# First attention: idle products in front of TensorE's waits, clearings and a first gate moved

## The chip, the cores and the metric

The kernel runs on one core of a Trainium2 chip. A core has a matrix engine (TensorE, PE in the profile), a vector engine (VectorE, DVE), an activation engine (ScalarE, ACT), a general engine (GpSimd, POOL) and a queue that issues transfers (SyncE, SP). The engines run their own instruction streams and wait for each other through semaphores. The metric is the device time of one launch in microseconds (us), and less is better.

## The reference

Six sublayers are added one after another to x (32 sequences of 64 tokens, 512 wide, so 2048 tokens), each on the layer norm of x. The change touches the first three:

```python
# 1: latent attention, 32 heads, latent width 4
C_q, C_kv = xn @ Wq_d + bq_d, xn @ Wkv_d + bkv_d
q = (C_q @ W_qk + b_qk).reshape(b, s, 32, 4)
attn = softmax(einsum('bqhd,bkd->bhqk', q, C_kv) / 2)
x += einsum('bhqk,bkhd->bqhd', attn, C_kv @ Wv_u + bv_u) @ Wo + bo
# 2: cross attention to ctx, 32 heads of 16 over 8 groups, mask added
x += softmax(xn_g @ ctx_g^T / 4 + mask) @ ctx_g
# 3: linear layer with 4 rank-8 experts, the expert by argmax of the gate logits
x += xn @ W_up^T + one_hot(argmax(xn @ gate_w^T + bias)) * lora(xn)
```

Then come a polynomial gated layer with a feed-forward part (4), one more attention (5) and a feed-forward layer with a latent branch (6). None of their code is changed.

## The kernel before

x lies in SBUF as 16 tiles of 128 tokens (`NT` = 16), in chunks of four tiles (`NC` = 4, `TC` = 4). Weights and activations are split into a high and a low fp16 half, and `mm3` (L116 to L118) multiplies them with three products. The order of each engine's work is written out by hand.

**Stage A, the first attention** (`stage_a`, until about 202 us). A unit is 16 heads of one tile; there are N = 32 units, eight in a chunk, n = 8c + j. TensorE's loop runs over n and issues `scores(n+1)` (L1118), `attend(n-2)` (many products of 10 columns, L116 to L118 into `a_p_v`), `scores_t(n)` (L1153), then the "front" work of the next chunk and the output work of the last one by the table `ring` (T: turn a normed tile, L: latents, V: values, Q: queries, Z: turn the result, O or P: output product; Y stands for Z by tiles in the last chunk), and last `turn_top(n+1)` (L1130). The other engines follow in the same order: VectorE takes the row maximum (`peak`, L603) and norms the result (`norm_z`), ScalarE does `shift` (L908), the exponential and the high half, GpSimd the low half (`low_p`, L435). On VectorE `spread` (L573) writes the masked keys of the next chunk and `low_query` (L595) the low half of a query block, which a later Q on TensorE waits for.

`keep_warm(times)` (L1137) issues products of 128 x 96 by 512 bf16 columns of an identity into `p_m`, whose rows 0 to 95 nobody reads: idle products, whose result is thrown away. Before the change 14 stand at the start (`EARLY_WARM`) and `light(c, j)` products behind the front work of an iteration, 0, 2 or 4.

GpSimd's `next_step(m)` prepares the second attention between the units: m = 0 and 1 clear `vn[0]` and `vn[1]` (L477), m = 2 writes a column of constants (L482), and later steps split its first keys and values.

**Stage B, the second attention** (`part_b`, about 202 to 367 us). It has again 32 units with the same kind of loop from n = -2: `turn` (L110), `scores`, `peak` (L1355), `shift` (L1526), `turn_p` (L1538), `attend`. `p_v`, the fourth bank of `p_y`, takes the results of `attend`. Stages A and B are separate blocks, and all engines meet between them.

**Stage C, the linear layer** (`part_c`, about 361 to 440 us). For a tile t, TensorE turns it (`trans`), forms gate logits and expert columns (`aux`) and the base product (`main`, twelve products of 512 columns); VectorE's `gate(t)` (five small instructions, L1639 to L1649) picks the expert, ScalarE's `high_z` and VectorE's `low_z` (L1655) split the picked columns, TensorE turns them (`turn_z`, L1775) and adds them (`delta`, L1781). `trans`, `aux` and `main` of tile 0 are issued inside stage B. Their results lie in other banks than `p_v`, but `main(1)` writes the bank of `p_v`.

## Time and profile before

| | |
|---|---|
| median of 3 runs | 1196.1 us (1193.16 to 1198.43) |
| the profiled execution's own time | 1192.04 us |
| its span | 1190.3 us |
| mean granted TensorE clock | 0.956 |
| PE busy | 1110.0 us, 93% of the span |
| DVE busy | 689.0 us, 58% |
| ACT busy | 492.6 us, 41% |
| POOL busy | 375.8 us, 32% |
| chain that ended last, by engine | PE 70%, DVE 9%, issue 2%, ACT 1% |

### The profile page before, as it was taken

How to read it: one execution, taken by the hardware profiler on the slowest of the kernel's cores; microseconds unless marked ns; L12 is line 12 of the kernel's file. 1: busy time of each engine (PE TensorE's matmuls, PEld its weight loads, DVE VectorE, ACT ScalarE, POOL GpSimd, SP SyncE). 2: the span in 40 equal slices, each digit the busy share in tenths (PEclk: the TensorE clock that was granted, in tenths of full speed). 3: DMA queues.
4: the chain of work that ended last, by engine and by line, in shares of the span. 5: the costliest groups of instructions: out<-in, count | busy, mean ns of one | idle time of the engine just before them, and what ended most of it. 6: DMA issues, size and time to landing. Idle time of an engine off the chain costs nothing.

```text
span 1190.3 us, 23660 instructions
## 1 busy us (share of the span) xinstructions
PE 1110.0 (93%) x9380; PEld 594.2 (50%) x9380; DVE 689.0 (58%) x1221; ACT 492.6 (41%) x871; POOL 375.8 (32%) x339
## 2 busy tenths in 40 slices
PE   7778996999998989999999999999989899999996
PEld 3444553677775444444444444444555544444442
DVE  6787775588887775335314412531389923656565
ACT  4465673788864644222212211221266622223221
POOL 2255465566651320000460160000043400415063
PEclk8888886799998999999999999999999999999998
DMA  7000000111120211310020010000000000000001
GB/s 242 2 2 4 18 15 9 41 47 45 44 68 4 83 47 43 107 62 1 21 81 1 0 53 0 1 1 1 0 12 10 1 1 1 18 18 26 9 29 43
DMA packets 29011, 35.91 MB, mean 30 GB/s; under 512 B 5882, under 2 KB 20499, under 8 KB 28788
## 3 DMA queue, kind: packets, MB, share of 16 engines
q1 hardware_dynamic: 27506, 34.53, 9.2%
q8 instruction: 67, 1.10, 0.4%
q10 hardware_dynamic: 1410, 0.06, 0.1%
q14 instruction: 28, 0.23, 0.1%
HBM read 30.24 MB, written 4.19 MB: 29 GB/s over the span
## 4 chain that ended last, share of the span: by engine, by line
PE 70%; DVE 9%; issue 2%; ACT 1%; POOL 0%; DVEq 0%; POOLq 0%; ACTq 0%
PE p_up L116 11%; PE p_up L117 11%; PE p_up L118 11%; PE p_y L116 9%; PE p_y L118 9%; PE p_y L117 9%; PE p_y L1538 3%; PE p_up L110 2%; DVE e_den L2257 2%; PE p_up L1526 1%; PE p_up L1503 1%; DVE wd_lo L103 1%; DVE st L188 1%; PE p_up L1508 1%; PE p_y L110 1%
## 5 line engine op out<-in xcount | busy, mean ns | idle before, releaser
L1949 DVE TENSOR_TENSOR d_h_low<-d_hf,d_h_high 128x512 f16<-128x512 f32 (+1 forms) x40 | 27.9, 697 | 205.1 <-ACT d_h_high L2038 205.1
L116 PE MATMUL p_up<-d_xt_high,wd_hi 128*128 128x512 f16 (+1 forms) x352 | 133.4, 379 | 2.9 <-PE p_y L118 1.5
L117 PE MATMUL p_up<-d_xt_low,wd_hi 128*128 128x512 f16 (+1 forms) x352 | 133.4, 379 | 0.0
L118 PE MATMUL p_up<-d_xt_high,wd_lo 128*128 128x512 f16 (+1 forms) x352 | 133.4, 379 | 0.0
L170 ACT ACTIVATE d_sg<-p_up 128x512 f32<-128x512 f32 (+1 forms) x40 | 23.8, 594 | 212.8 <-PE p_up L118 212.7
L116 PE MATMUL p_y<-wd_hi,d_h_high 128*128 128x512 f16 (+1 forms) x272 | 103.1, 379 | 0.0
L117 PE MATMUL p_y<-wd_lo,d_h_high 128*128 128x512 f16 (+1 forms) x272 | 103.1, 379 | 0.0
L118 PE MATMUL p_y<-wd_hi,d_h_low 128*128 128x512 f16 (+1 forms) x272 | 103.1, 379 | 0.0
L435 POOL TENSOR_TENSOR a_pt_low<-a_ex,a_pt_high 128x1024 f16<-128x1024 f32 x32 | 68.1, 2127 | 80.3 <-ACT a_pt_high L924 80.2
L138 POOL TENSOR_SCALAR wd_raw<-wd_raw 128x1156 f32<-128x1156 f32 x8 | 25.1, 3140 | 207.1 <-DVE d_h_low L1949 207.1
L2219 POOL TENSOR_TENSOR wd_hi<-wd_hi,e_den 128x1024 f32<-128x1024 f32 x16 | 30.5, 1909 | 147.7 <-DVE e_den L2259 147.7
L2549 DVE TENSOR_TENSOR d_h_low<-d_hf,d_h_high 128x512 f16<-128x512 f32 x32 | 28.6, 893 | 66.1 <-ACT d_h_high L2647 66.1
L116 PE MATMUL p_up<-d_xt_high,wf_hi 128*128 128x512 f16 x160 | 61.2, 382 | 0.0
L117 PE MATMUL p_up<-d_xt_low,wf_hi 128*128 128x512 f16 x160 | 61.1, 382 | 0.0
L118 PE MATMUL p_up<-d_xt_high,wf_lo 128*128 128x512 f16 x160 | 61.0, 381 | 0.0
L116 PEld LDWEIGHTS p_up<-d_xt_high,wd_hi 128*128 128x128 f16 (+1 forms) x352 | 35.3, 100 | 44.7 <-issue 3.0
L2640 ACT ACTIVATE d_sg<-p_up 128x512 f32<-128x512 f32 x32 | 19.1, 596 | 88.9 <-PE p_up L118 88.9
L118 PEld LDWEIGHTS p_up<-d_xt_high,wd_lo 128*128 128x128 f16 (+1 forms) x352 | 35.3, 100 | 40.7
L117 PEld LDWEIGHTS p_up<-d_xt_low,wd_hi 128*128 128x128 f16 (+1 forms) x352 | 35.3, 100 | 40.1
L1294 POOL TENSOR_TENSOR wd_lo<-wd_lo 128x512 f16<-128x512 f32 x30 | 34.7, 1157 | 45.7 <-ACT wd_lo L1437 41.1
L116 PE MATMUL p_y<-wf_hi,d_h_high 128*128 128x512 f16 x128 | 48.5, 379 | 0.1
L117 PE MATMUL p_y<-wf_lo,d_h_high 128*128 128x512 f16 x128 | 48.5, 379 | 0.0
(340 smaller groups left out, 2890.6 us busy)
## 6 DMA issues: line engine op xcount, KB each, us to landing
wd_raw<-in_w_d SPq DMA_DIRECT2D x16, 616.0 KB, 3.7
wd_raw<-in_w_f SPq DMA_DIRECT2D x8, 578.0 KB, 3.8
X<-in_x SPq DMA_DIRECT2D x4, 1024.0 KB, 12.3
wd_lo<-in_ctx_t SPq DMA_DIRECT2D x128, 32.0 KB
out_x<-wd_raw SPq DMA_DIRECT2D x16, 256.0 KB, 2.0
wd_lo<-in_ctx SPq DMA_DIRECT2D x32, 64.0 KB, 2.4
wd_raw<-in_w_c SPq DMA_DIRECT2D x1, 1096.0 KB, 12.5
wd_hi<-in_Wo SPq DMA_DIRECT2D x1, 1024.0 KB
```

The lines of the kernel that those rows point to most:

```text
L110: last = nc.tensor.transpose(ps[:, 128 * k:128 * k + 128], xn[:, 128 * k:128 * k + 128], held.ident[:])
L116: nc.tensor.matmul(ps, st[0], mv[0], start=start, stop=False)
L117: nc.tensor.matmul(ps, st[0], mv[1], start=False, stop=False)
L118: return nc.tensor.matmul(ps, st[1], mv[0], start=False, stop=stop)
L138: nc.gpsimd.tensor_scalar(raw, raw, WS, None, ALU.mult).then_inc(done, 1)
L435: nc.gpsimd.tensor_tensor(pt[1][:, n % 3, :, :], ex[:, n % 2, :, :], pt[0][:, n % 3, :, :], ALU.subtract).then_inc(pt_ready, 1)
L1294: nc.gpsimd.tensor_tensor(bd[1][:, h, :, 128 * i:128 * i + 128], ks.rearrange("p (k n) -> p k n", k=KB), bd[0][:, h, :, 128 * i:128 * i + ...
L1538: last = nc.tensor.transpose(p_t[:, q, 128 * k:128 * k + 128], prob[:, n % 2, 8 * q + 2 * k:8 * q + 2 * k + 2, :] .rearrange("p h k -> p ( ...
L1949: nc.vector.tensor_tensor(hid[1][0:n, d % NH, :], value, hid[0][0:n, d % NH, :], ALU.subtract).then_inc(h_ready, 1)
L2219: nc.gpsimd.tensor_tensor(prob[:, t % 3, :, :], prob[:, t % 3, :, :], den[:, t % 2, :].rearrange("p (j a) -> p j a", a=1).broadcast_to([12 ...
L2257: nc.vector.tensor_reduce(den[:, b, :], prob[:, t % 3, :, :], AX.X, ALU.add).then_inc(sum_ready, 1)
L2549: nc.vector.tensor_tensor(hid[1][:, f % NH, :], sq[:, f % 2, :], hid[0][:, f % NH, :], ALU.subtract).then_inc(h_ready, 1)
```

## The change

Idle products are added in stage A: 30 in place of 14 at the start; 7 behind `scores(0)` and 6 behind `turn_top(0)`; 7 in place of 2 at the end of iterations 4 and 6; 6 at the head of iteration 7; 2 ahead of the front work of iterations 12, 13, 20 and 21; 5 and 4 ahead of `attend` in the two iterations after the last unit; 5 ahead of the third output block of the last chunk and 2 ahead of its fourth. In stage B a `keep_warm` of its own (128 x 128 by 512 columns, into `p_v`) is added: 8 ahead of `turn(0)`, 5 ahead of `turn(1)`, 5 ahead of `shift(0)`. GpSimd's clearings move from behind `low_p` of units 12, 14 and 16 to those of units 10, 18 and 19. Stage C's `gate(0)` moves from the head of stage C on VectorE into stage B's iteration 31, `high_z(0)` on ScalarE ahead of `norm(2)`, and on TensorE `trans(2)`, `aux(1)` and `main(1)` go ahead of `turn_z(0)`, with a wait for stage B's last result (`held.b_outputs`) ahead of `main(1)`.

```diff
@@ -343,7 +343,9 @@
         def bank(use):
             return p_f[:, bank_of[use], :]
 
-        EARLY_WARM = 14
+        EARLY_WARM = 30
+        WAITS = {4: 7, 6: 7}
+        TAIL = {N: 5, N + 1: 4}
         held.rs_steps = 4 * NC - 2
 
         def light(c, j):
@@ -477,7 +479,7 @@
                         nc.gpsimd.memset(vn[m], 0.0).then_inc(next_clear, 1)
                     elif m == 2:
                         pool.wait_ge(next_clear, 2)
-                        pool.wait_ge(pt_ready, N - 15)
+                        pool.wait_ge(pt_ready, N - 12)
                         for r, h in halves:
                             nc.gpsimd.memset(vn[0][r, :, :, h, DH:DH + 1], AS).then_inc(next_clear, 1)
                         pool.wait_ge(next_clear, 4)
@@ -515,8 +517,8 @@
                         pool.wait_ge(next_low, 2)
                 for n in range(N):
                     low_p(n)
-                    if n in (12, 14, 16):
-                        next_step((n - 12) // 2)
+                    if n in (10, 18, 19):
+                        next_step({10: 0, 18: 1, 19: 2}[n])
                     if 24 <= n < 31:
                         next_step(n - 21)
                     if n in (2, 5):
@@ -1186,27 +1188,39 @@
                     if use[0] == "Q" and use[2] == 1:
                         fold_bvo(range(2, 4))
                 scores(0)
+                keep_warm(7)
                 turn_top(0)
+                keep_warm(6)
                 for use in second:
                     front(use)
                 for n in range(N + 2):
+                    if n == 7:
+                        keep_warm(6)
                     if n + 1 < N:
                         scores(n + 1)
+                    if n in TAIL:
+                        keep_warm(TAIL[n])
                     if n >= 2:
                         attend(n - 2)
                     if n < N:
                         scores_t(n)
+                        if n // 8 in (1, 2) and n % 8 in (4, 5):
+                            keep_warm(2)
                         for use in chunk_uses(n // 8, n % 8):
                             front(use)
-                        keep_warm(light(n // 8, n % 8))
+                        keep_warm(WAITS.get(n, light(n // 8, n % 8)))
                     else:
                         for use in after[n]:
+                            if use == ("P", NC - 1, 2):
+                                keep_warm(5)
                             front(use)
                     if n + 1 < N:
                         turn_top(n + 1)
                     if n % 8 == 1 and n // 8 + 1 < NC and n < N:
                         latents(n // 8 + 1, range(2, KB))
                 for use in final:
+                    if use[0] == "P":
+                        keep_warm(2)
                     front(use)
 
 
@@ -1247,6 +1261,7 @@
         held.rs_c = rs_at
         held.rs_steps += 2 * NC
         held.b_done = v_ready, VW + N
+        held.b_outputs = z_ready, N
         if True:
             def sync(sp):
                 def fetch(c, i):
@@ -1400,6 +1415,8 @@
                     if n == N - 2:
                         p.c.low(v, 0)
                         p.c.low(v, 1)
+                    if n == N - 1:
+                        p.c.gate(v, 0)
                     if n + 2 < N:
                         peak(n + 2)
                     if n >= 0 and n % 2 == 0 and n // 2 + 2 < NT:
@@ -1555,11 +1572,21 @@
                                            [w[:, 2 * (t % TC) + s, 2 * k + slot, :, :].rearrange("p h n -> p (h n)")
                                             for w in vb], True, True)
                     last.then_inc(v_ready, 1)
+                def keep_warm(times):
+                    for _ in range(times):
+                        nc.tensor.matmul(p_v, held.ident16[:],
+                                         held.ident16[:].rearrange("p (a n) -> p a n", a=1).broadcast_to([128, 4, 128]),
+                                         start=True, stop=True)
+
+                keep_warm(8)
                 turn(0)
+                keep_warm(5)
                 turn(1)
                 for n in range(-2, N + 1):
                     if 0 <= n < N:
                         turn_p(n)
+                    if n == -1:
+                        keep_warm(5)
                     if 0 <= n + 1 < N:
                         shift(n + 1)
                     if n + 2 < N:
@@ -1671,7 +1698,7 @@
         for t in range(NT):
             if t:
                 update(v, t - 1)
-            gate(v, t)
+                gate(v, t)
             if 1 <= t < NT - 1:
                 low(v, t + 1)
             low_z(v, t)
@@ -1726,8 +1753,8 @@
 
         nc.scalar.activation(ident_h[:], held.ident[:], ACT.Copy).then_inc(ident_ready, 1)
         nc.scalar.activation(held.lora[0:3 * RZ, :], held.lora_raw[0:3 * RZ, :], ACT.Copy, scale=BS).then_inc(lora_hi, 1)
+        high_z(act, 0)
         norm(act, 2)
-        high_z(act, 0)
         for t in range(1, NT):
             copy_z(act, t - 1)
             if t + 1 < NT:
@@ -1781,7 +1808,13 @@
         nc.tensor.matmul(p_out(t), zt[:, t % 2, :], held.lora[0:3 * RZ, :], start=False, stop=True).then_inc(out_ready, 1)
 
     def tensor(pe, turn_next):
-        for t in range(1, NT):
+        trans(pe, 2)
+        aux(pe, 1)
+        pe.wait_ge(*held.b_outputs)
+        main(pe, 1)
+        turn_z(pe, 0)
+        delta(pe, 0)
+        for t in range(2, NT):
             turn_z(pe, t - 1)
             if t + 1 < NT:
                 trans(pe, t + 1)
@@ -1795,7 +1828,7 @@
         turn_next(2)
         delta(pe, NT - 1)
         turn_next(3)
-    p.low, p.norm, p.trans, p.high, p.aux, p.main = low, norm, trans, high, aux, main
+    p.low, p.norm, p.trans, p.high, p.aux, p.main, p.gate = low, norm, trans, high, aux, main, gate
     p.gpsimd, p.vector, p.scalar, p.tensor = gpsimd, vector, scalar, tensor
     return p
```

## Rows read from the trace of the kernel before

**Rows 1.** The page, part two: granted TensorE clock in 40 slices, in tenths.
```profile
PEclk8888886799998999999999999999999999999998
```

**Rows 2.** Windows: stretch, length, busy us (instructions) by engine, clock, DMA share, GB/s.
```profile
12.90:19.60 6.70, 5.59 (x14) 3.33 (x15) 4.09 (x16) 2.28 (x3) 0.00 (x0) 0.50 1.03 392
36.50:43.60 7.10, 4.36 (x24) 2.96 (x25) 5.45 (x9) 1.62 (x4) 0.00 (x0) 0.52 0.00 0
64.30:67.50 3.20, 3.20 (x38) 2.08 (x36) 3.00 (x8) 1.91 (x3) 0.25 (x1) 0.50 0.03 8
74.40:81.30 6.90, 6.01 (x65) 3.88 (x66) 4.64 (x10) 3.22 (x5) 1.11 (x1) 0.51 0.01 2
108.60:125.60 17.00, 16.82 (x144) 9.38 (x143) 12.16 (x18) 10.44 (x15) 7.37 (x5) 0.50 0.01 2
146.00:159.50 13.50, 13.45 (x96) 5.81 (x98) 9.86 (x15) 7.39 (x10) 4.24 (x2) 0.50 0.16 44
190.40:221.00 30.60, 21.15 (x190) 11.75 (x188) 11.78 (x21) 10.78 (x17) 11.28 (x15) 0.50 0.09 26
367.90:374.60 6.70, 2.91 (x21) 1.93 (x22) 3.89 (x13) 1.13 (x3) 3.32 (x8) 0.50 0.01 2
228.00:352.00 124.00, 124.00 (x2990) 93.62 (x2990) 109.74 (x185) 101.06 (x157) 79.92 (x105) 1.00 0.19 53
```

**Rows 3.** Waits of PE, 0:205 and 205:500: us in total, times, longest us.
```profile
PE a_p_m L1130 <- DVE a_top L603: 7.0, 4, 2.4
PE a_p_f L1029 <- DVE a_qs L595: 4.7, 4, 2.6
PE a_p_st L1075 <- DVE wd_hi L684: 4.1, 1, 4.1
PE a_p_s L1118 <- DVE a_bd L573: 2.2, 1, 2.2
PE a_p_f L110 <- DVE a_xn L103: 2.2, 2, 2.0
...
PE p_y L1775 <- DVE c_zcat L1655: 8.8, 7, 4.9
```

**Rows 4.** Idle products: timeline (start, us), then the tile view (ns min/median/max).
```profile
3.92 5.96 PE L1137 MATMUL a_p_m<-ident 128*96 128x512 bf16 x14 [3.92 <-DVE ident L803]
54.01 1.06 PE L1137 MATMUL a_p_m<-ident 128*96 128x512 bf16 x4
...
L1137 PE MATMUL a_p_m<-ident x54: 377/381/662, 3.9 to 186.4; 128*96 128x512 bf16 x54
```

**Rows 5.** Timeline of PE: scores of units 13, 14, 15 and 16.
```profile
98.22 0.62 PE L1118 MATMUL a_p_s<-a_bd,a_qs 96*64 96x512 f16 x4
...
102.69 0.62 PE L1118 MATMUL a_p_s<-a_bd,a_qs 96*64 96x512 f16 x4
...
109.47 1.06 PE L1118 MATMUL a_p_s<-a_bd,a_qs 96*64 96x512 f16 x4
...
115.04 1.06 PE L1118 MATMUL a_p_s<-a_bd,a_qs 96*64 96x512 f16 x4
```

**Rows 6.** Timeline of all engines, 100:110: a spread beside a clearing.
```profile
102.34 4.00 DVE L573 TENSOR_SCALAR a_bd<-a_keys,mask_a 96x512 f16<-96x512 f16 x1
...
104.28 1.91 POOL L477 MEMSET wd_lo<- 128x2176 f16 x1
```

**Rows 7.** Timeline of PE and DVE, 199:236: stage B's first tile and four maxima.
```profile
202.74 1.11 PE L110 MATMUL p_y<-ident,d_xn 128*128 128x128 f32 x4 [2.83 <-DVE d_xn L103]
...
210.18 1.22 DVE L1355 TENSOR_REDUCE b_top<-p_up 128x16 bf16<-128x1024 f32 x1 [2.38 <-PE p_up L118]
216.24 1.23 DVE L1355 TENSOR_REDUCE b_top<-p_up 128x16 bf16<-128x1024 f32 x1 [4.84 <-PE p_up L118]
...
226.02 1.22 DVE L1355 TENSOR_REDUCE b_top<-p_up 128x16 bf16<-128x1024 f32 x1 [0.39 <-PE p_up L118]
...
230.38 1.23 DVE L1355 TENSOR_REDUCE b_top<-p_up 128x16 bf16<-128x1024 f32 x1 [0.32 <-PE p_up L118]
```

## The prediction

> **What bounds the kernel now.** I read the page's clock line first. It stands at 8 tenths in the first six slices and at 6 and 7 in slices seven and eight; from slice nine on it is nearly full, with one 8 at slice 13 [rows 1]. So the clock is lost in the first attention and just behind it. Narrow windows then gave the stretches at 1.2 GHz: 6.7, 7.1, 3.2, 6.9, 17.0, 13.5 and 30.6 us up to 221, and 6.7 us more at 368, together 91.7 us [rows 2]. Each row has to be read for what else was busy. Between 108.6 and 125.6 TensorE has work for 16.82 of 17.00 us: it sets the pace there, and a faster clock shortens it. Between 64.3 and 67.5 VectorE is busy for 3.00 of 3.20, so a faster TensorE gains next to nothing. In the stretch from 228 to 352 TensorE is busy for all 124 us at full clock [rows 2]: stage B is bound by it, and a lead at its start is kept to its end.
>
> The table of waits shows what the idle products are put in front of: four waits for a row maximum (7.0 us, longest 2.4), four for a query's low half (4.7, longest 2.6), one of 4.1 at the start, one of 2.2 for a spread, two for a normed tile (2.2), and 4.9 ahead of stage C's first `turn_z` [rows 3]. In all but the last a clock at half rate follows or overlaps them.
>
> **What an idle product costs.** At 1.2 GHz 14 of them take 5.96 us, 0.43 each. Four at full clock take 1.06; a single one has a median of 0.38, so they follow each other by (1.06 - 0.38) / 3 = 0.23 us [rows 4]. The change adds 69 in stage A (16 + 7 + 6 + 5 + 5 + 6 + 8 + 5 + 4 + 5 + 2) and 18 in stage B: 87, which is 20 us of TensorE at full clock and 37 at half. They cost nothing only inside a wait whose end another engine sets.
>
> **Part by part.** *Start.* The 14 products end at 9.88, the wait ends at 14.0. The last of them already has the short duration (the minimum of 377 ns is near; the 662 is the cold form [rows 4]), so 16 more take 16 x 0.23 = 3.7 us and end by 13.6: hidden. What follows ran at half clock from 12.9 to 19.6 with TensorE busy for 5.59. Upper bound: half of it, 2.8. VectorE has only 2.6 us of idle time there [rows 2], and the norm of the third tile waits for a turn in it; behind, it runs without a gap to the first keys. Lower bound 0. I take 1.5.
>
> *First unit.* 7 products (1.6) stand in a wait of 2.3 and 6 (1.4) in one of 2.0, so both are hidden. Behind, 36.5 to 43.6: TensorE 4.36, so at most 2.2; VectorE's idle part is 1.65 [rows 2]. I take 1.4 (bounds 0 and 2.2).
>
> *Iterations 4, 6 and 7.* 5, 5 and 6 more products (1.15, 1.15, 1.4) in waits of 2.4, 2.1 and 2.2 [rows 3]: hidden. The stretch at 64 us gives 0 for the reason above. The one from 74.4 to 81.3 has TensorE at 6.01 (at most 3.0) and VectorE idle for 2.3 [rows 2]; ScalarE's copies of the turned tiles come next. I take 1.7 (bounds 0 and 2.3).
>
> *The clearing.* `spread` at 102.34 takes 4.00 us and ends with GpSimd's clearing, which runs from 104.28 for 1.91 [rows 6]. Behind it stands the query's low half, for which TensorE waits 2.6 [rows 3]. With the clearing behind `low_p(10)`, where VectorE then works from PSUM, the spread would wait for `low_p` alone: 1.9 gained (bounds 0 and 2.0). The other two moved steps go to units in whose gaps no spread stands; should one be met there, it costs the same 1.9. Sentences on the skill: the Trainium skill, page "SBUF — State Buffer", section "Who interferes with whom", says that the second of two instructions of VectorE and GpSimd that contend for the shared ports is blocked until the first has finished. By that rule taken alone the spread would have gone on when `low_p` ended, the clearing behind it would be harmless, and this term would be 0 in place of 1.9; the row, which ends with the clearing, speaks against it, and I go by the row.
>
> *Chunks two and three.* Two units of the same kind of work (a query and an output block): scores 13 to 14 take 102.69 - 98.22 = 4.47 us at full clock, scores 15 to 16 take 115.04 - 109.47 = 5.57 at half [rows 5]. Each such unit gives 1.1. The stretch of 17.0 holds 17.0 / 5.57 = 3.05 units, so 3.4, less 0.5 since one of them turns two tiles while VectorE's norm is held up by GpSimd: 2.9. The stretch of 13.5 holds 2.4 units: 2.7. Bounds: 0, if the clock falls all the same, and VectorE's idle part, 4.8 and 3.6 [rows 2]. The 8 added products (1.8) stand ahead of queries that wait for their low halves (4.7 us in four waits [rows 3]): hidden. Without that cover, and with the waits that the clearing caused gone, they cost up to 1.8 at full clock.
>
> *Tail of stage A.* In it GpSimd's low halves and VectorE's normed tiles release TensorE; 5 + 4 + 5 + 2 products (3.7 us at full clock) stand in those waits. The last two output blocks, 8 products of 512 columns, run at half clock in the chain: 8 x (0.43 - 0.23) = 1.6, and the turn between them 0.2: 1.8 (bounds -1 and 1.8).
>
> *Start of stage B.* All engines meet at 202; `turn(0)` starts at 202.74 on a normed tile [rows 7], so there is 0.6 us of cover for 8 products. At full clock they take 1.8 and delay it by 1.1, at half clock 3.4 and by 2.8. Against that, maxima follow each other by 216.24 - 210.18 = 6.06 us at half clock and by 230.38 - 226.02 = 4.36 later [rows 7]. Three groups of scores lie in the stretch: 3 x 1.7 = 5.1. The two turns give 1.0 more. Less 1.1 for the products and 0.5 for ScalarE, whose key work before the first exponential is next: 4.5. The two groups of 5 fit ahead of `turn(1)` and `shift(0)` (1.2 us each in waits of 1.5 and 1.3). Bounds: half of TensorE's 21.15 busy us less the tail [rows 2], some 8, and -2.8.
>
> *Stage C.* TensorE stands idle for 4.9 us until `low_z(0)` and drops to half clock [rows 3]. With the gate early, `trans(2)`, `aux(1)` and `main(1)` (about 3.5 us) fill that hole. The gate's five instructions (1.1 us) now hold up VectorE's `norm_o(30)`, so the last `attend` starts some 0.75 later. And `low_z(0)` still stands behind the last statistics on VectorE, so `turn_z(0)` comes only 0.7 earlier. What is gained is that `main(1)` is done and nothing runs at half clock: stage C's cycle, delta to update to gate to `turn_z`, starts 1.8 earlier. Bounds: -0.8 (the delay alone) and 4.9. I take 1.8.
>
> **Sum.** 1.5 + 1.4 + 0 + 1.7 + 1.9 + 2.9 + 2.7 + 1.8 + 4.5 + 1.8 = 20.2 us. Off the profiled execution's 1192.0 that is 1171.8. That execution is 4.1 below the median of the runs shown (1196.1), so the median should be 1175.9; I say 1176. Stages behind stage C see the same work, only earlier.
>
> **Rivals.** *The chain takes over.* In the full-clock units VectorE and ScalarE are already nearly serial with TensorE, and the saved time turns into waits for a maximum or a low half. Then 1.7, 2.9 and 2.7 go, and half of the first two terms (1.4): the gain is 20.2 - 8.7 = 11.5 and the time 1184.6. For it: VectorE is busy for 12.16 of 17.00. Against: the 4.47 at full clock is itself measured. *The clock falls all the same* in the tail and at stage B's start, where waits for GpSimd, the meeting of the engines and 10-column products leave TensorE with little, and in one of the two long stretches. Then 1.8 and 2.7 go, and of 4.5 there remains 1.5 (products at half clock, but the clock back before 221): the gain is 12.7 and the time 1183.4. *Slower.* The idle products run at half clock and outlast the waits: 16 x 0.43 = 6.9 against 4.1, 7 and 6 against 2.3 and 2.0 (+1.3), 6 against 2.2 (+0.4), 8 with no cover (+3.4), the tail's 16 (+1.9), stage B's 18 (+4.2): +14.0 us, less 1.9 for the clearing and 1.8 for stage C, so 1206. It decides once a product takes more than about 0.3 us on average. Against it: the product at 9.5 us was already short [rows 4]. *All comes back.* If TensorE set the pace in every stretch, half of 91.7 would go: 45.9, and the time 1150. The skill has this as a rule: the Trainium skill, "TensorE: Matmul & The Clock Gate", section "HAM oscillation — how this bites in real kernels", puts the penalty at half of the throttled time. VectorE's 3.00 of 3.20 and TensorE's 2.91 of 6.70 [rows 2] contradict it for two of the eight stretches at least.
>
> **Chances.** Forecast 0.55, chain 0.17, clock 0.20, slower 0.04, all back 0.02, no effect 0.02. A difference of 0.5% (6.0 us) is what a measurement of this kernel can tell from none: faster 0.92, same 0.04, slower 0.04. The range reaches from 1168 (the bounds of the start of stage B and of stage C) to 1189, which takes in both middle rivals.
>
> **What would show it.** Right: granted clock 1.00 from about 10 to 360 us with at most one dip; no `spread` longer than 2.2 us; unit periods of 4.5 or less in iterations 14 and 22; `turn_z(0)` with a wait under 1 us; stage B's first maxima 4.4 apart. Wrong: idle products of 0.43 us anywhere behind 10 us, `turn(0)` more than 2 us behind its normed tile, or VectorE waits of TensorE as long as before at full clock.

## The result, and the profile after

The changed kernel takes 1183.65 us (median of 4 runs, 1181.75 to 1186.04) against 1197.26 for the kernel before on the same chip: a ratio of 0.9912, 95% interval [0.9888, 0.9936], some 10.5 us (the two medians, of four runs each, lie 13.6 apart). A second measurement, in the rounds of later experiments, gave 1183.83 against 1193.12, 0.9926 [0.9901, 0.9952], 8.8 us. So it is faster, as forecast, and within the range of 1168 to 1189, but by about half of the 20.2 us of the sum. The profiled execution took 1186.04 us with a span of 1184.3, which is 6.0 less than the span before.

The clock line of the page after, to be held against [rows 1]:

```profile
PEclk9899999999999999999999999999999999999998
```

The 6s and 7s are gone. The windows at six places of [rows 2] (same columns), with three more where the clock now falls (24:44, 84:92, 428:440). It also falls inside 108.6:125.6 and 146:159.5:

```profile
12.90:19.60 6.70, 5.54 (x25) 3.30 (x26) 5.66 (x20) 4.60 (x8) 0.00 (x0) 1.00 1.02 383
24.00:44.00 20.00, 18.16 (x82) 7.33 (x81) 12.91 (x30) 3.80 (x7) 0.00 (x0) 0.66 0.00 1
74.40:81.30 6.90, 5.28 (x86) 3.48 (x85) 6.72 (x11) 3.37 (x7) 1.80 (x2) 1.00 0.01 2
84.00:92.00 8.00, 7.34 (x41) 2.84 (x42) 2.79 (x6) 4.20 (x7) 4.00 (x2) 0.79 0.01 2
108.60:125.60 17.00, 13.62 (x175) 8.56 (x171) 14.66 (x19) 12.02 (x18) 7.92 (x4) 0.90 0.00 1
146.00:159.50 13.50, 10.94 (x130) 5.81 (x130) 11.94 (x17) 7.30 (x10) 5.84 (x3) 0.87 0.11 32
190.40:221.00 30.60, 26.53 (x352) 15.33 (x352) 16.32 (x27) 16.16 (x27) 12.58 (x19) 0.94 0.12 33
428.00:440.00 12.00, 9.22 (x40) 4.25 (x39) 5.93 (x13) 2.18 (x5) 1.27 (x2) 0.86 0.01 3
228.00:352.00 124.00, 123.02 (x2926) 93.45 (x2926) 109.72 (x186) 97.41 (x152) 74.77 (x98) 1.00 0.17 50
```

Two of these rows carry the surprise. In 108.6:125.6 TensorE was busy for 16.82 of 17.00 us before; now it is at 13.62, and VectorE went from 12.16 to 14.66. TensorE no longer sets the pace there. VectorE's busy time includes the time in which an instruction of it is held up, as the `spread` below. And the last row, full clock before and after, shows 123.02 where it showed 124.00: stage B now has a pause of about 1 us in it.

TensorE's waits after, 0:205 and 205:500 (as [rows 3]):

```profile
PE a_p_m L1139 <- DVE ident L805: 3.9, 1, 3.9
PE a_p_s L1120 <- DVE a_bd L575: 3.8, 2, 1.9
PE a_p_m L1132 <- DVE a_top L605: 3.3, 3, 1.5
PE a_p_st L1155 <- ACT a_qs L910: 2.8, 7, 1.0
PE p_y L1577 <- PEq L356: 2.4, 1, 2.4
PE a_p_f L1031 <- DVE a_qs L597: 2.4, 6, 0.6
...
PE p_y L1802 <- DVE c_zcat L1682: 6.4, 7, 2.5
...
PE p_y L116 <- issue: 1.0, 1, 1.0
```

The waits for maxima and low halves are shorter, as they should be with products in front of them. The second line is the new one: two waits of 1.8 and 1.9 us for a `spread`, ahead of `scores(16)` and `scores(24)`. The first of them in the timelines of PE, DVE and GpSimd, with the scores as in [rows 5] and the spread as in [rows 6]:

```profile
103.77 0.62 PE L1120 MATMUL a_p_s<-a_bd,a_qs 96*64 96x512 f16 x4
108.41 0.62 PE L1120 MATMUL a_p_s<-a_bd,a_qs 96*64 96x512 f16 x4
112.67 0.28 PE L1132 MATMUL a_p_m<-ident,a_top 128*8 128x128 bf16 x2
114.78 0.62 PE L1120 MATMUL a_p_s<-a_bd,a_qs 96*64 96x512 f16 x4 [1.83 <-DVE a_bd L575]
...
111.41 1.22 DVE L605 TENSOR_REDUCE a_top<-a_p_s 128x16 bf16<-128x1024 f32 x1
112.54 2.15 DVE L575 TENSOR_SCALAR a_bd<-a_keys,mask_a 96x512 f16<-96x512 f16 x1
...
112.41 2.12 POOL L437 TENSOR_TENSOR a_pt_low<-a_ex,a_pt_high 128x1024 f16<-128x1024 f32 x1 [2.52 <-ACT a_pt_high L926]
```

Scores 14 to 15 take 108.41 - 103.77 = 4.64 us (6.78 before): the spread of 4.00 us is gone. (All seven profiles with the clearings in their old places have one of 3.99 to 4.01 us; in the others no spread takes more than 2.26.) Scores 15 to 16 take 6.37, although at full clock, where they took 5.57 at half clock [rows 5]. TensorE is done with `turn_top` at 113.0 and waits for a spread that lies beside `low_p`: it starts 0.13 behind it, takes 2.15 us where one alone takes 0.34, and ends at 114.69, 0.16 behind `low_p`. Here the lock rule weighed in the prediction (the Trainium skill, "SBUF — State Buffer", "Who interferes with whom": the second one waits until the first has finished) agrees with the row.

The start of stage B, timeline of PE and the maxima on DVE (as [rows 7]; PEq is TensorE's sequencer):

```profile
197.67 3.25 PE L1577 MATMUL p_y<-ident 128*128 128x512 bf16 x8 [2.37 <-PEq L356]
200.71 0.96 PE L110 MATMUL p_y<-ident,d_xn 128*128 128x128 f32 x4
...
205.89 1.22 DVE L1370 TENSOR_REDUCE b_top<-p_up 128x16 bf16<-128x1024 f32 x1 [0.73 <-PE p_up L118]
209.86 1.23 DVE L1370 TENSOR_REDUCE b_top<-p_up 128x16 bf16<-128x1024 f32 x1 [2.75 <-PE p_up L118]
213.84 1.23 DVE L1370 TENSOR_REDUCE b_top<-p_up 128x16 bf16<-128x1024 f32 x1 [1.03 <-PE p_up L118]
```

The eight products start 2.37 us into the wait, take 3.25 us and outlast it; behind `turn(0)` the first maxima follow each other by 3.97 us, where the first two followed by 6.06.

### The profile page after: what moved, and what is told of

Same layout as the page of the kernel before. It is cut to its first block, busy times and chain, and to the rows that moved or that the text cites. A ratio compares the mean times of both kernels' runs of the same rounds, so it can differ in the third digit from the quotient of the medians.

```text
span 1184.3 us, 23834 instructions
## 1 busy us (share of the span) xinstructions
PE 1115.3 (94%) x9467; PEld 593.7 (50%) x9467; DVE 691.0 (58%) x1221; ACT 492.1 (42%) x871; POOL 376.3 (32%) x339
## 4 chain that ended last, share of the span: by engine, by line
PE 70%; DVE 9%; issue 2%; ACT 1%; POOL 0%; DVEq 0%; POOLq 0%; ACTq 0%
PE p_up L116 11%; PE p_up L117 11%; PE p_up L118 11%; PE p_y L116 9%; PE p_y L117 9%; PE p_y L118 9%; PE p_y L1555 3%; DVE e_den L2290 2%; PE p_up L110 2%; PE p_up L1543 1%; DVE wd_lo L103 1%; PE p_up L1520 1%; DVE st L188 1%; PE p_up L1525 1%; PE p_y L110 1%
## 5 line engine op out<-in xcount | busy, mean ns | idle before, releaser
L118 PE MATMUL p_y<-wf_hi,d_h_low 128*128 128x512 f16 x128 | 48.5, 379 | 0.0
```

The lines of the kernel that those rows point to most:

```text
L118: return nc.tensor.matmul(ps, st[1], mv[0], start=False, stop=stop)
```

## The experiments

All ratios are to the kernel before, in runs on the same chip. The long table further down shows where each kernel's profile spends its time.

**Each part alone.** Four kernels are the kernel before with one part of the change. Their edits are the hunks of the diff: e1_gate those of stage C, e2_clear the two on GpSimd's clearings, e3_prod_a stage A's 69 products, e4_prod_b stage B's 18.

e1_gate. 

> Only stage C's part of the change (gate(0), high_z(0), and trans(2), aux(1), main(1) ahead of turn_z(0)). Theory (a clock dip in stage C takes the gain back): 0 to 1 us faster than before. Rival (the term of the prediction stands, and the loss lies elsewhere): 1.8 us faster, the wait for turn_z(0) under 1 us.

Measured: 1.0031 [1.0014, 1.0048], 3.7 us slower: neither. In the table below stage C is 0.7 us shorter (82.56 for 83.21), but the start of stage four takes 37.36 us at a mean clock of 0.91, where it took 34.58 at 1.00.

e2_clear. 

> Only GpSimd's clearings moved. Theory (the spread of 4.00 us was held by the clearing): 1.5 to 2.5 us faster, the longest spread about 2.2 us. Rival (the spread is held for as long anyway, or another spread or norm meets a clearing in its new place): within 0.5 us of before.

Measured: 0.9969 [0.9951, 0.9988], 3.7 us faster, more than the theory said; the longest spread is 2.22 us.

e3_prod_a. 

> Only stage A's 69 idle products. Theory (the faster clock is turned into waits of TensorE for VectorE's spreads and into other dips): 3 to 5 us faster than before. Rival (the prediction's sum for stage A less the clearing): 12 us faster.

Measured: 1.0002 [0.9983, 1.0022], no gain: neither.

e4_prod_b. 

> Only stage B's 18 idle products. Theory (as in the changed kernel's trace: 2.8 us for products at half clock ahead of turn(0), then a group of scores each 1.7 us shorter): 3 to 4 us faster. Rival (without stage A's products the clock is at half rate and the 18 products outlast their waits): 0 to 4 us slower.

Measured: 1.0008 [0.9990, 1.0025], within the rival's 0 to 4 us slower. But stage B's start is as short as in the changed kernel (19.31 for 25.39 us); what the kernel loses lies elsewhere.

The four sum to about +1 us, the whole to -9 or -10: the parts do not add up. The windows 100:126 of e2_clear, then of e3_prod_a, show who does the work in chunk two:

```profile
100.00:126.00 26.00, 21.73 (x269) 12.72 (x265) 20.04 (x27) 16.80 (x24) 11.24 (x6) 0.93 0.00 1
```
```profile
100.00:126.00 26.00, 22.57 (x205) 12.06 (x202) 20.45 (x24) 15.33 (x21) 14.31 (x10) 0.67 0.00 1
```

Without a single added product, moving the clearings lifts the granted clock of chunk two to 0.93 and lets TensorE get through 269 matmuls; with all of stage A's products and the clearings in their old places it is 0.67 and 205, no better than in the kernel before (0.67 and 206). The wait of 2.6 us for the low half [rows 3] is not in e2_clear; its longest there is 0.8.

**The whole again, and without one part.**

e8_whole is the changed kernel. 

> The changed kernel itself once more, on the chip and in the rounds of the experiments beside it. Theory (the parts work only together: products of the first attention hold the clock into stage B, where stage B's products then find it high): ratio to the kernel before 0.989 to 0.994, and the profile again without the long half clock behind 190 us, but with short falls in other places of the first attention than the first profile of it had (there 24 to 44, 84 to 92, 116 to 120, 152 to 160). Rival (the parts add up, and the first measurement was kind to the change): 0.997 to 1.001, the sum of the four parts. If the falls of the first attention stand in the same four places, they are caused by its code and not by chance.

Measured: 0.9926 [0.9901, 0.9952]. Of the four falls of the first profile, the long one (24 to 44 us) is not there and that of 84 to 92 lies two units earlier (72 to 80); the two behind `scores(16)` and `scores(24)` are there again, at 112 to 116 and 148 to 152. So those two stand in the code, and the other two change from one execution to the next.

e9_no_gate leaves stage C as before. 

> The changed kernel with stage three's first gate and its idle products left as they were before: idle products of stages A and B and the clearings only. Theory (the part on stage three loses as much here as alone, 0.3%): 3 to 4 us faster than the whole change, ratio 0.986 to 0.989. Rival (it gains its 1.8 us of the forecast inside the whole, and was slow alone only because what lies ahead of it was at another phase): 1 to 2 us slower than the whole.

Measured: 0.9923 [0.9899, 0.9947], the same as the whole. The gate part is worth nothing here; neither number came.

e10_prods has stage A's and B's products and nothing else. 

> Idle products of stages A and B together, with GpSimd's clearings and stage three's gate as before. Alone the two parts gave 0.02% and 0.08% against (ratios 1.0002 and 1.0008). Theory (they work only together, since the falls at the end of the first attention and at the begin of stage B are one): ratio 0.994 to 0.997, and in the profile turn(0) to the fifth scores of stage B in 19.3 us with at most 4 us of half clock between 188 and 224 us. Rival (the clearing is what lets the products work, since its 2.7 us wait ahead of iteration 14 stays bare): 0.999 to 1.002.

Measured: 0.9972 [0.9955, 0.9988], at the edge of what the theory said. So the two sets of products, worth nothing each, give 3.3 us together. But they do not do so where the theory looks. From the last scores of the first attention to the fifth of stage B, e3_prod_a gains 2.6 us on the kernel before, e4_prod_b 3.3 and e10_prods 5.7: there they simply add up. What eats the gain of each alone lies elsewhere. Behind stage B (C, D start and the rest of the span), whose code is the same in all of them, the kernel before takes 836.1 us, e3_prod_a 841.3, e4_prod_b 841.8 and e10_prods 838.6. Why is open. The clearings on top are worth 0.0049 (0.9972 to 0.9923), against 0.0031 alone, a difference within the noise.

**The start.**

```diff
                 for use in first:
+                    if use == ("Q", 0, 1):
+                        keep_warm(7)
```

e7_start. 

> The changed kernel with seven more idle products (1.5 us at full clock) in the wait of 1.84 us ahead of the front of queries (0,1), at 26.4 us. Theory (that wait is where the clock fell and then stayed low until 43.5 us, which made the first scores 2.2 us later than before): clock 1.00 from 24 to 44 us, first scores at about 32.3 us as in the kernel with the first attention's products alone, and 2 to 4 us faster than the whole change. Rival (the fall there is chance: the kernel with only the first attention's products has the same wait of 1.84 us and no fall): the same time within 1 us, whatever its profile shows there.

Measured: 0.9894 [0.9870, 0.9918], 1180.76 us, as the theory said, though the interval overlaps that of the whole. The row 24:44 of e7_start, to be held against that of the kernel after above (0.66):

```profile
24.00:44.00 20.00, 16.88 (x118) 8.60 (x117) 17.23 (x38) 7.94 (x13) 2.10 (x1) 1.00 0.01 1
```

In ten profiles of kernels with the change's start, five show a fall here (`scores(1)` at 39.9 to 43.3 us) and five none (38.6 to 38.8). In the four with the seven products it is at 38.5 to 39.1. The wait of 1.84 us is a place where the clock falls in some executions and not in others; four profiles are too few to show that the seven products prevent it.

**The eight products ahead of turn(0).** e5_no8 deletes `keep_warm(8)`, e12_4of8 makes it 4.

e5_no8. 

> The changed kernel without the eight idle products ahead of turn(0) of stage B; the other ten products of that stage stay. Theory (they begin at 2.4 us into the wait, run at half clock and outlast it: the wait of 2.83 us of the kernel before becomes 5.8 us): from the last scores of the first attention to turn(0) 20.9 instead of 23.5 us; the products behind turn(0) still bring the clock back before the fifth scores, so the kernel is 1.5 to 2.8 us faster than the whole change. Rival (the eight are what brings the clock back): turn(0) comes earlier, but the clock stays low past 212 us, turn(0) to the fifth scores takes 21.5 us or more instead of 19.2, and the time is that of the whole change or up to 1 us above it.

Measured: 0.9912 [0.9889, 0.9935], 1182.58 us.

e12_4of8. 

> The changed kernel with four idle products ahead of turn(0) of stage B instead of eight. Theory (they start 2.37 us into the wait of 2.83 us and run at half clock at 0.40 us each, so that each one beyond the first delays turn(0) by its length): from the last scores of the first attention to turn(0) 21.9 to 22.2 us (eight: 23.0 to 23.5, none: 20.9), and 0.8 to 1.5 us faster than the whole change. Rival (the products there bring the clock back for stage B's first scores, so that fewer of them lose there what they save here): turn(0) to the fifth scores of stage B 20 us or more instead of 19.3, time as the whole change.

Measured: 0.9906 [0.9883, 0.9928], 1181.51 us. From the last scores of the first attention to `turn(0)`: 20.89 (none), 21.69 (four), 23.02 and 23.49 (eight). From there to the fifth scores: 19.91, 19.53, 19.31 and 19.21, so none of them is the rival's 20 or more. The eight cost 2.1 to 2.6 us and bring 0.6 to 0.7. By the medians e5_no8 is 1.25 us faster than e8_whole, but their intervals overlap. PE's timeline of e5_no8, `turn(0)` and the five products behind it:

```profile
194.86 1.12 PE L110 MATMUL p_y<-ident,d_xn 128*128 128x128 f32 x4 [2.83 <-DVE d_xn L103]
195.77 2.34 PE L1577 MATMUL p_y<-ident 128*128 128x512 bf16 x5
```

**The spread.** e6_spread_act takes the spreading of chunks two to four from VectorE to ScalarE:

```diff
-                    if more and 3 <= j < 7:
-                        spread(c + 1, range(j - 3, j - 2))
...
+                        nc.scalar.activation(bd[0:PR, c % 2, :, h, :], keys[0:PR, :].rearrange("p (b k) -> p b k", k=S),
+                                             ACT.Copy, scale=held.mask_a[:, h:h + 1]).then_inc(bd_ready, 1)
```

> The changed kernel with the spreading of the keys of chunks two to four moved from VectorE to ScalarE; nothing else. Theory (in the chunks' first iterations the last spreading is held on VectorE for 2.2 us beside GpSimd's low_p, TensorE waits 1.8 to 1.9 us for it ahead of scores(16) and scores(24), and the clock falls there): both waits gone, from scores(14) to scores(22) 35.5 to 36.5 us instead of 37.6, scores(22) to (30) likewise 1 to 2 us shorter, and 2 to 4 us faster than the whole change. Rival (ScalarE is the busier engine in these iterations and its exponentials now wait for the spreadings): the two waits turn into waits for ScalarE in the four iterations ahead of them, time unchanged or 1 to 3 us worse.

Measured: 0.9904 [0.9882, 0.9926]. PE's waits, 95:170:

```profile
PE a_p_s L1127 <- ACT a_bd L972: 3.5, 2, 1.7
```

The wait changed its engine and hardly its length: ScalarE's spread takes 0.71 us but stands behind the query's copy. Neither price is right; the kernel is within the noise of the whole.

e15_early leaves it on VectorE and issues the fourth one an iteration earlier:

```diff
-                    if more and 3 <= j < 7:
-                        spread(c + 1, range(j - 3, j - 2))
+                    if more and 3 <= j < 6:
+                        spread(c + 1, range(j - 3, j - 2) if j < 5 else range(2, 4))
```

> The changed kernel with the fourth spreading of each of chunks two to four one iteration earlier (iteration 5 of a chunk issues two, iteration 6 none), still on VectorE. Theory (scores(16) and scores(24) wait because the last spreading stands behind the maxima of the iteration right ahead of them, and is held there beside low_p; on ScalarE it stood behind the front and ended at the same time): the waits for a_bd of 1.83 and 1.94 us are gone or under 0.5 us, scores(15) to scores(16) 5.0 to 5.4 us instead of 6.37, and 1.5 to 3 us faster than the whole change. Rival (behind that wait stands the next one, for the low half of the queries or for the shift): the wait is renamed and at least 1.2 us long, time within 1 us of the whole change.

Measured: 0.9900 [0.9880, 0.9920], 1180.15 us. PE's waits of e15_early, 95:170:

```profile
PE a_p_f L1031 <- DVE a_qs L597: 2.7, 5, 0.9
PE a_p_f L110 <- DVE a_xn L103: 1.0, 1, 1.0
PE a_p_st L1155 <- ACT a_qs L910: 0.6, 2, 0.4
```

The two waits for `a_bd` are gone, as the theory said, and scores 15 to 16 take 5.60 us in place of 6.37, but scores 14 to 22 take 37.97, no less than the 37.7 with them: the time went into other waits of the same units, for the low half and for a normed tile. Scores 22 to 31 are 0.6 shorter. Whether the rest of the 3 us against e8_whole is real (the intervals overlap) is open.

**Products between the first units and the tail.** e18_no467 takes the added ones out of iterations 4, 6 and 7.

> The changed kernel without its new idle products in iterations 4, 6 and 7 (iterations 4 and 6 have their two each as before, iteration 7 none); all else stays. Theory (they delay what stands behind them in more units than they speed up, since the stretch at half clock which they remove lies beside VectorE and ScalarE): scores(1) to scores(14) 57.5 to 59.5 us instead of 60.5, and 1 to 2 us faster than the whole change, ratio 0.991 or less. Rival (they hold the clock there, as the prediction had it): 61 to 62 us for that stretch, half clock in it for 7 us and more, and 1 to 2 us slower.

Measured: 0.9883 [0.9860, 0.9906], 1180.58 us. The time is the theory's, the reason is not. The stretch from `scores(1)` to `scores(14)` in e18_no467 and then in the kernel after:

```profile
40.25:101.10 60.85, 52.38 (x622) 29.73 (x621) 46.30 (x91) 40.37 (x55) 30.32 (x18) 0.86 0.02 3
```
```profile
43.28:103.77 60.49, 52.62 (x638) 29.53 (x638) 46.94 (x91) 40.30 (x55) 30.34 (x18) 0.97 0.02 3
```

With a mean clock of 0.86 (some 17 us at half) this stretch takes 60.85 us, with 0.97 it takes 60.49: all in all the clock bought 0.4 us. The kernel is about 5 us faster than e8_whole by the ratios, 3.5 us than the first measurement of the same kernel; 1 to 2.5 of them are the pause of the next experiment, which it does not have.

What sets the length of the stretch can be read unit by unit. Scores 7 to 8 take 4.6 us in five of the twenty profiles (e0_before, e1_gate, e2_clear, e17_count, e19_lean) and 6.1 to 8.4 us in the other fifteen, among them all that have the products of iterations 4, 6 and 7. One small instruction of VectorE (L740, five columns) goes with it, here in e0_before and then in the kernel before:

```profile
67.93 0.15 DVE L740 TENSOR_TENSOR wd_hi<-wd_hi 128x5 f32<-128x5 f32 x1
68.28 2.15 POOL L435 TENSOR_TENSOR a_pt_low<-a_ex,a_pt_high 128x1024 f16<-128x1024 f32 x1 [4.17 <-ACT a_pt_high L924]
```
```profile
68.27 2.13 POOL L435 TENSOR_TENSOR a_pt_low<-a_ex,a_pt_high 128x1024 f16<-128x1024 f32 x1 [3.71 <-ACT a_pt_high L924]
68.38 2.03 DVE L740 TENSOR_TENSOR wd_hi<-wd_hi 128x5 f32<-128x5 f32 x1
```

Ahead of `low_p` it takes 0.15 us; 0.11 behind its start it takes 2.03 and ends with it, and the maximum, the norm and the spread of that unit stand behind it. In the five short profiles it starts 0.26 to 0.35 us ahead of `low_p`, in the fifteen long ones 0.1 to 1.3 behind. The five are also those in which TensorE is at half clock all through scores 6 to 7 (4.61 us, in most others 4.35 with more of it at full clock). So a clock that is kept up there seems to bring `low_p` ahead of this instruction and to lose 2.6 us for the 0.3 that it gains. That is read from the rows; no run moved the instruction.

**The pause in stage B.** e17_count adds 87 small products to the kernel before, at its very begin:

```diff
                 keep_warm(EARLY_WARM)
+                for _ in range(87):
+                    nc.tensor.matmul(p_m[96:104, 0:16], held.ident16[:, 0:8], held.ident16[:, 0:16], start=True, stop=True)
```

> The kernel before with 87 more small products (8 stationary and 16 moving columns) on TensorE behind the 14 at its very begin, in its wait of 4.1 us there; nothing else. They are as many instructions as the idle products of stages A and B. Theory (the pause for 'issue' in stage B, at scores 24 to 27, comes from how many instructions TensorE has been given ahead of that place, not from the clock): a pause of 0.7 to 1.3 us for 'issue' between 325 and 345 us, and 0 to 2.4 us lost there. Rival (it comes with reaching that place sooner, ahead of transfers that are under way): no pause, as in the kernel before. The time otherwise as before, within 1 us, or 1 to 2 us better if these products keep the clock up at the start.

Measured: 1.0042 [1.0022, 1.0062]. The timeline of PE in e17_count, in e8_whole and in the kernel after:

```profile
334.34 0.20 PE L116 MATMUL p_y<-wd_lo,wf_hi 128*64 128x34 f16 x1 [0.71 <-issue]
```
```profile
325.44 0.20 PE L116 MATMUL p_y<-wd_lo,wf_hi 128*64 128x34 f16 x1 [0.71 <-issue]
```
```profile
331.58 0.20 PE L116 MATMUL p_y<-wd_lo,wf_hi 128*64 128x34 f16 x1 [0.98 <-issue]
```

It stands in the same unit each time, between `scores(27)` and `scores(28)`, with no wait for another engine, and it comes with the number of instructions ahead of it: all eleven profiles with 79 to 87 added ones have it (0.7 to 1.6 us, in five of them with a fall of the clock right behind), and none of the nine with 0, 18, 62, 69, 71 or 94. Why these instructions come late is not shown by these traces. The 4.8 us that e17_count is slower are not explained by it; its profile, among its fastest runs, took 841.0 us behind stage B, where the kernel before took 836.1 and 836.4.

**A second profile of the kernel before.** e0_before. 

> The kernel before once more, for a second profile of it. The first profile was, from the fifth scores of stage B to the start of stage four's loop, 2 to 3 us shorter than in five other kernels whose stage three is the same or nearly so. Theory (the granted clock of the code behind stage B falls in one place more or less by chance, and the first profile was a lucky one): from the fifth scores of stage B to the first wait of stage four for d_xt_low 213 us or more instead of 211.7, and the first attention (first scores to last) within 3 us of 145.5. Rival (a kernel that reaches stage B sooner meets more falls behind it): 211 to 212 us again.

Measured: 0.9994 [0.9978, 1.0011]. From the fifth scores of stage B to the wait for `d_xt_low` it took 212.0 us: the rival's number, so the two profiles of this kernel agree. But e2_clear, whose stage C is the same code, takes 84.78 + 36.20 us there, where these two take 83.2 to 83.5 + 34.58: the code alone does not fix it. And the first attention went otherwise: scores 1 to 14 in 58.3 us, not 61.2.

**Together.** e13_both is e7_start and e5_no8 in one kernel.

> The changed kernel with the seven products at the start added and the eight ahead of turn(0) taken out. Theory (the two gains lie in different places and add up): 1.2 us (without the eight) and 3 us (with the seven) faster than the whole change, so a ratio to before of 0.987 to 0.990. Rival (without the eight the clock comes back later in some runs, which takes back the gain): 0.990 to 0.993, no better than with the seven alone.

Measured: 0.9876 [0.9856, 0.9896], 1179.74 us, as the theory said and the lowest ratio, though the intervals of the next ones overlap it.

e16_best is e13_both with e15_early's edit.

> The three edits that paid or should pay in one kernel: seven products at the start, none ahead of turn(0), the fourth spreading an iteration earlier. Theory: the gain of e15_early on top of ratio 0.9876, so 0.985 to 0.9868. Rival (with the wait gone TensorE only reaches the chain of the next iteration sooner): 0.987 to 0.989.

Measured: 0.9889 [0.9865, 0.9913], 1180.17 us: the rival.

e19_lean is e13_both without the added products in iterations 4, 6 and 7 and in chunks two and three.

> e13_both without the idle products in iterations 4, 6 and 7 and without the eight in chunks two and three. What stays of the change: the start, the first unit, the clearings, the tail, ten products in stage B, stage three's gate. Theory (in the chunks the clearing does the work: scores(14) to scores(22) took 37.5 us with the clearings and without any product of the first attention, 42.1 with products and without the clearings): scores(14) to scores(22) 37.4 to 38 us, and the time that of e13_both or 1 to 2 us below, ratio 0.986 to 0.988. Rival (without products in the chunks the clock falls in them and the wait behind takes longer): 39 us or more there and a ratio of 0.989 or more.

Measured: 0.9880 [0.9856, 0.9904], 1179.89 us, with 62 added products in place of 86: the theory's ratio. Scores 14 to 22 took 38.5 us, between the two numbers, and 22 to 31 took 38.2 (35.8 with them). So the products may hold something in chunk three, but e2_clear has none of them and took 35.55; what leaving them out costs here comes back as the pause that is gone and as scores 1 to 14 in 58.2.

**Where the time is, by profile.** us, worked out from the starts of the rows in each timeline: first scores of unit 1; from scores 1 to 14, 14 to 22, 22 to 31; to `turn(0)`; to the fifth scores of stage B; to the 31st exponential of stage B; to the 16th copy in stage C; to the first activation of stage four's loop. Behind it a kernel takes 718.2 to 719.1 or 720.7 to 720.9, whatever was changed. Six more profiles, not shown, go into the means below.

| | s1 | 1-14 | 14-22 | 22-31 | turn(0) | B start | B | C | D start | span |
|---|---|---|---|---|---|---|---|---|---|---|
| before | 41.49 | 61.20 | 40.78 | 36.38 | 22.89 | 25.39 | 126.08 | 83.21 | 34.58 | 1190.3 |
| e0_before | 41.05 | 58.34 | 41.98 | 36.61 | 22.79 | 28.62 | 126.06 | 83.48 | 34.58 | 1191.8 |
| e1_gate | 41.44 | 57.54 | 43.55 | 36.88 | 22.83 | 25.29 | 126.08 | 82.56 | 37.36 | 1192.6 |
| e2_clear | 41.56 | 57.39 | 37.45 | 35.55 | 22.89 | 25.19 | 126.07 | 84.78 | 36.20 | 1185.4 |
| e3_prod_a | 38.56 | 60.40 | 42.12 | 35.69 | 20.91 | 24.80 | 126.08 | 84.49 | 36.06 | 1189.8 |
| e4_prod_b | 41.29 | 62.09 | 44.21 | 36.87 | 25.69 | 19.31 | 126.04 | 84.76 | 36.18 | 1197.3 |
| e10_prods | 39.88 | 60.48 | 43.58 | 36.37 | 23.25 | 19.31 | 128.67 | 83.21 | 34.58 | 1190.2 |
| after | 43.28 | 60.49 | 37.69 | 35.76 | 23.49 | 19.21 | 127.28 | 82.57 | 36.22 | 1184.3 |
| e8_whole | 38.77 | 59.72 | 37.55 | 35.70 | 23.02 | 19.31 | 128.57 | 82.48 | 36.04 | 1181.9 |
| e9_no_gate | 38.70 | 60.44 | 37.58 | 35.81 | 23.21 | 19.31 | 128.87 | 83.16 | 34.58 | 1182.5 |
| e7_start | 38.50 | 60.49 | 37.69 | 35.73 | 23.49 | 19.20 | 126.06 | 83.53 | 36.27 | 1179.4 |
| e5_no8 | 40.05 | 60.49 | 37.68 | 35.75 | 20.89 | 19.91 | 127.20 | 82.59 | 34.58 | 1177.4 |
| e18_no467 | 40.25 | 60.85 | 37.68 | 35.70 | 23.49 | 19.21 | 126.03 | 83.56 | 36.27 | 1181.4 |
| e19_lean | 39.06 | 58.23 | 38.47 | 38.21 | 20.15 | 19.96 | 126.10 | 82.57 | 36.12 | 1179.7 |

Read it by columns: columns 14-22 and B start each fall into two groups, with and without the clearings, with and without stage B's products. Column 1-14 shows how much one and the same code varies: before, e0, e1 and e4 do the same work there in 57.5 to 62.1 us.

## Why the prediction was right in its direction and wrong in its size

The step that failed is the price of a unit at half clock: **a TensorE that is busy in such a unit sets the pace there, so that the full clock gives back 1.1 us of it** (2.9 and 2.7 us for the stretches of 17.0 and 13.5 us, and in the same way 1.7 for the one at 74 us). The price came from one pair of units, scores 13 to 14 and 15 to 16, that differ in more than the clock. Measured, the very unit that took 5.57 us at half clock takes 6.37 at full clock, since TensorE then waits 1.83 us for a spread that VectorE can't finish beside `low_p`. In e16_best, at full clock and without that wait, it takes 4.73, so some 0.8 us were there to be had; but scores 14 to 22 take 39.04 us in it, against 37.7 in the kernel after, since the next units are longer. In place of 2.7 us chunk three gave 0.5, and in place of a gain of 1.7 the units up to `scores(14)` lost 1.4. Two more terms were mis-sized: stage B was to keep the lead of its start and lost 2.2 us to a pause of its own, and stage C gave 0 in place of 1.8.

What was right is the direction, the spread held by the clearing, and the tail of stage A with the start of stage B. The text's own signs tell the same: the first maxima came less than 4.4 us apart, no spread took more than 2.25 us (the text said 2.2) and `turn_z(0)` had no wait. But in the kernel after, the seven idle products at 37.5 us take 3.22 us, 0.46 each, and the eight ahead of `turn(0)` delay it by 2.1 to 2.6 us (e5_no8): two of the signs that it had named for being wrong.

Term by term, as means over the profiles that have the code in question and those that don't (so many of each), in us:

- *Start and first unit*, forecast 2.9: scores(1) goes from 41.4 (5) to 39.7 (10), 1.7. Where the clock holds it is 2.7 and the forecast is met; in five of ten executions it falls at 27 us all the same.
- *The stretch at 74 us* (iterations 4, 6, 7), forecast +1.7: scores 1 to 14 go from 59.1 (6) to 60.6 (9), -1.4. This is a term with the wrong sign. Leaving the products out again (e18_no467, 60.85) does not bring it back; what goes with it is the VectorE instruction shown there, held 1.5 us or more beside `low_p`, and a fall of the clock that makes scores 2 to 3 or 10 to 11 some 1.7 us longer in eleven of the fourteen profiles with the changed start and in none of the other six. The half-clock stretch of the profile before [rows 2] was in part an accident of that execution: e0_before has none at 74 us.
- *Clearing and chunk two*, forecast 1.9 + 2.9: scores 14 to 22 go from 42.4 (7) to 37.6 (9), 4.8. That the sum is right is luck, since its division is not: e2_clear has all of it and the products (e3, e10) have none. Without the clearing beside the spread the wait of 2.6 us for the low half [rows 3] is gone, and of the 17 us at half clock behind it some 3 remain. Against the profile before alone it is 3.1.
- *Chunk three*, forecast 2.7: scores 22 to 31 go from 36.3 (6) to 35.8 (10), 0.5. The rival "the chain takes over" is what happens here: the wait for the spread of 1.9 us is new, and behind it the next ones stand (e15_early).
- *Tail and start of stage B*, forecast 1.8 + 4.5: `turn(0)` 0.5 later (22.85 to 23.3), stage B's start 6.5 shorter (25.8 to 19.3), together 6.0. Stage A's products alone bring `turn(0)` 1.9 us earlier (e3_prod_a 20.91), as forecast (1.8). The eight ahead of it then delay it by 2.4 and not by 1.1, and what they help to bring behind it is 6.5. Without them the two terms would be 7.8.
- *Stage B behind its start*, forecast 0 ("a lead at its start is kept to its end"): 126.1 to 128.2 (6 profiles of the changed kernel and its variants with 87 added ones), -2.2. The prediction put this at nothing and did not count instructions.
- *Stage C*, forecast 1.8: the stage takes 83.1 (12) in place of 83.9 (8), but the start of stage four 36.2 in place of 35.3, since with the early gate the clock falls there in eleven of twelve profiles, else in four of eight. Together 0.0. `turn_z(0)` lost its wait of 4.9 us, and `turn_z(1)` got one of 2.5: half of the hole moved by a tile.

Sum: 1.7 - 1.4 + 4.8 + 0.5 + 6.0 - 2.2 + 0 = 9.4 us, against 9.3 by the medians of e8_whole and 8.8 by its ratio; the two values behind stage four's start are not in it. The 10.8 that are missing from 20.2 are 1.2, 3.1, 0, 2.2, 0.3, 2.2 and 1.8.

The rivals. "The chain takes over" gave 1184.6 and "the clock falls all the same" 1183.4, both near to the measured 1183.65 to 1183.83. The first holds for the terms at 74 us and of chunk three, though not for chunk two. The second leaves 1.5 us for the tail and the start of stage B, where 6.0 were measured, although the clock does fall there for 3 to 4 us; elsewhere it holds, at 27 us in half of the profiles. "All comes back" is refuted: by the mean clock, time at half clock went from 2 x 0.044 x 1190.3 = 105 to 2 x 0.020 x 1184.3 = 47 us and the span by 6. Half of those 58 us, as the rule of the Trainium skill has it ("TensorE: Matmul & The Clock Gate", "HAM oscillation — how this bites in real kernels"), would be 29, as an estimate; here it is no more than an upper bound.

What stays open: why the clock falls at 27 us in one execution and not in the next; why the instructions come late at the pause in stage B, and why e17_count loses 4.8 us by the median; why e3_prod_a and e4_prod_b lose behind stage B what they gain ahead of it; whether the VectorE instruction, put elsewhere, would give its 2.6 us; and what makes the two values, 2.4 us apart, behind stage four's start.

## What to carry to other kernels

A stretch at half clock is worth what its slowest other engine leaves, and it can be enough to take away the wait in front of it: here moving GpSimd's clearings did in chunk two (37.45 us in e2_clear) what 87 idle products did not (43.58 in e10_prods). Ask also what the faster clock brings side by side: VectorE and GpSimd lost here, by a change of half a microsecond in their order, what TensorE had gained. Price such a change on several profiles of the kernel before, since where the clock falls differs from one execution to the next, and on those places the sum of a single profile is a draw. And count idle instructions as instructions: 62 of them did as well as 86.

## What the runs showed of the hardware that was not expected

- A pause of 0.7 to 1.6 us for "issue" on TensorE in a fixed unit of the code, which comes with 79 to 87 instructions more ahead of it and not with 0 to 71 or 94.
- A VectorE instruction of 128 x 5 elements takes 0.15 us when it starts ahead of GpSimd's `low_p` and 2.03 us when it starts 0.11 us behind it.
- A wait of 1.84 us on TensorE at 26 us is followed by a fall of the granted clock in five of ten profiles of the same code, once for 14 us and four times for 3 to 4.
- Eight idle products that begin at half clock take 3.25 to 3.57 us, five at full clock 1.25: as a cover for a wait they are only cheap where the clock is already up.
